# Attention outputs and sums of the third diagonal step, formed together with those of the fourth

## What is computed

```
q = (x @ Wq).reshape(B, S, N_KV, GROUP, HEAD_DIM)      # 4, 2048, 4, 4, 32
k = (x @ Wk).reshape(B, S, N_KV, HEAD_DIM)
v = (x @ Wv).reshape(B, S, N_KV, HEAD_DIM)
scores = jnp.einsum('bqkgd,bskd->bkgqs', q, k) * scale
scores = jnp.where(causal, jnp.finfo(scores.dtype).min, scores)
attn = jax.nn.softmax(scores, axis=-1)
out = jnp.einsum('bkgqs,bskd->bqkgd', attn, v)
```

## Time and profile before

| | |
|---|---|
| Median of 3 runs | 3938.41 us (3938.09 to 3940.97) |
| Profiled execution | 3937.35 us, its span 3935.6 us |
| PE busy | 3749.8 us (95%) |
| DVE busy | 2348.5 us (60%) |
| ACT busy | 1637.1 us (42%) |
| POOL busy | 1644.0 us (42%) |
| Mean granted TensorE clock | 0.973 |

### The profile page before, as it was taken

How to read it: one execution, slowest core, us unless ns; L and a number is a source line. 1 busy time by engine, 2 the same in 40 slices (tenths; PEclk the granted TensorE clock), 3 DMA queues, 4 the chain that set the end, 5 groups by cost and what they waited for, 6 DMA issues and landing times. The chain is left out here.

```text
span 3935.6 us, 71470 instructions
## 1 busy us (share of the span) xinstructions
PE 3749.8 (95%) x20752; PEld 2276.7 (58%) x20752; DVE 2348.5 (60%) x5385; ACT 1637.1 (42%) x3340; POOL 1644.0 (42%) x1412
## 2 busy tenths in 40 slices
PE   6999999999979979999999999999999999999889
PEld 5777787778854545545455444445454454544377
DVE  5454554445521128877787787778677676875144
ACT  3222222222211111555555555556555565655511
POOL 0424333242342310555555465555455455555600
PEclk9999999999999985999999999999999999999989
DMA  5232322323229972112202211210221021020086
GB/s 162 94 110 95 112 93 93 117 89 112 83 81 328 324 207 44 29 32 53 48 12 55 49 32 32 53 47 17 51 50 39 24 53 48 15 53 7 12 298 224
DMA packets 228463, 342.08 MB, mean 87 GB/s; under 512 B 65120, under 2 KB 77664, under 8 KB 228128
## 3 DMA queue, kind: packets, MB, share of 16 engines
q1 hardware_dynamic: 200480, 307.92, 25.4%
q0 software_dynamic: 17920, 12.82, 1.6%
q10 hardware_dynamic: 9728, 17.30, 1.2%
HBM read 217.28 MB, written 120.35 MB: 86 GB/s over the span
## 5 line engine op out<-in xcount | busy, mean ns | idle before, releaser
L1120 ACT ACTIVATE prb<-sps 128x512 f32<-128x512 f32 (+3 forms) x2560 | 1197.2, 538 | 903.4 <-PE sps L1238 890.8
L1153 DVE TENSOR_REDUCE mx<-mps 128x1 f32<-128x512 f32 x1536 | 1002.1, 682 | 204.0 <-PE mps L1215 204.0
L1215 PE MATMUL mps<-kst,qst 96*128 96x512 f32 (+2 forms) x2560 | 1011.2, 411 | 46.2 <-DMA kst<-k_hi_s 20.8
L1063 POOL TENSOR_TENSOR psum<-prb 128x1024 f32<-128x1024 f32 x384 | 908.5, 2381 | 292.7 <-ACT prb L1120 246.7
L1238 PE MATMUL sps<-qst,kst 97*128 97x512 f32 (+2 forms) x2560 | 967.1, 394 | 45.8 <-issue 20.4
L1238 PEld LDWEIGHTS sps<-qst,kst 97*128 97x128 f32 x2560 | 480.7, 191 | 440.9 <-ACT prb L1120 213.1
L1215 PEld LDWEIGHTS mps<-kst,qst 96*128 96x128 f32 x2560 | 502.1, 198 | 379.2 <-DVE mx L1153 202.3
L294 POOL DMA_INDIRECT tab_s<-pay,slot x384 | 380.0, 989 | 787.2 <-DVE tokf L543 667.1
L1156 DVE CUSTOM_DVE_ANT_0 mps<-mps,bias 128x256 f32<-128x256 f32 (+3 forms) x1024 | 523.3, 522 | 300.7 <-PE mps L1215 300.1
L1252 PE MATMUL ops<-prb,vst 128*32 128x512 f32 (+3 forms) x5120 | 599.5, 540 | 0.5 <-POOL prb L1053 0.5
L581 PE MATMUL acc<-x_hi,w_hi 128*128 128x512 f32 (+1 forms) x1152 | 457.1, 397 | 1.5 <-DVE x_lo L428 1.5
(11 more groups left out here) (154 smaller groups left out, 3194.6 us busy)
## 6 DMA issues: line engine op xcount, KB each, us to landing
wgu<-in_e_gu SPq DMA_DIRECT2D x32, 1408.0 KB, 7.3
qst<-q_hi_s SPq DMA_DIRECT2D x128, 256.0 KB, 4.5
x_sb<-in_x SPq DMA_DIRECT2D x16, 1024.0 KB, 7.4
xn_s<-xn SPq DMA_DIRECT2D x16, 1024.0 KB, 5.1
y_sb<-in_x SPq DMA_DIRECT2D x16, 1024.0 KB, 5.2
q_hi_s<-qk_hi SPq DMA_DIRECT2D x16, 1024.0 KB, 4.2
q_lo_s<-qk_lo SPq DMA_DIRECT2D x16, 1024.0 KB, 6.6
base<-y_sb SPq DMA_DIRECT2D x16, 1024.0 KB, 4.4
```

The costliest lines, as they stand in the source:

```text
L1063: nc.gpsimd.tensor_tensor(psum2[gi % 2][pr][:], prb[:, (2 * f + pr) % RP], prb[:, (2 * (f + 1) + pr) % RP], ALU.add).then_inc(add_done, 1)
L1120: nc.scalar.activation(prb[:, (2 * k + h // 2) % RP, h % 2, q0:CH], sps[:, (GROUP * k + h) % R, q0:CH], ACT.Exp, scale=SCALE).then_inc(exp ...
L1153: V.tensor_reduce(mx[:, h * NKT + qt, j:j + 1], mps[:, n % R, 0:wr], AX.X, ALU.max).then_inc(mred_done, 1)
L1215: M(out[:, 0:w], qst[p][0:R3, h, qt * P:(qt + 1) * P], kst[p][0:R3, k0:k0 + w], start=True, stop=True).then_inc(m_done, 1)
```

## The change

In step k TensorE formed the outputs of step k - 2. Now a list `due` says which outputs each step forms. Where step k - 2 is a third diagonal one (r = 2), its outputs are left out of step k and stand in step k + 1, ahead of those of the fourth diagonal step. For a group's last block, where k - 2 is negative, this holds across the group's end. Pieces, scores and all other engines' programs keep their order.

```
+            due = [[k - LAG] for k in range(NK)]
+            for k in range(NK):
+                if steps[k - LAG][2] == 2:
+                    due[k + 1] = due[k] + due[k + 1]
+                    due[k] = []
+
             def group(bg, p, nxt, prev=True):
...
-                    if k >= LAG:
-                        output(bg, p, k - LAG)
-                    elif prev:
-                        output(bg - 1, 1 - p, NK + k - LAG)
+                    for o in due[k]:
+                        if o >= 0:
+                            output(bg, p, o)
+                        elif prev:
+                            output(bg - 1, 1 - p, NK + o)
```

## The result

The changed kernel takes 3947.9 us (median of 17 runs, 3944.11 to 3948.85), the kernel before 3937.16 in the same runs (17, 3933.94 to 3943.71). The ratio is 1.0025 with a 95% interval of 1.0018 to 1.0032: 7 to 13 us slower, 10.7 by the medians. The profiled execution took 3948.48 us with a span of 3946.7.

A forecast was written before the change was run, and what follows sets the result against it. TensorE was taken as the attention stage's bound on average, VectorE and ScalarE following closely. Per group 0.27 + 0.24 + 0.17 - 0.07 = 0.61 us, together 9.2 us, gave 3947.5 us, range 3930 to 3956.

The forecast's parts named there:

- The price of a stretch: Attention stage, TensorE: one stretch of outputs costs 0.33 us beyond its columns; 63 merged would give 21 us.
- only the switches count: Rival for the merged blocks: VectorE and ScalarE keep up, so 21 us faster, 3917; chance 0.12.
- the crossing: Steps 0 and 1, last block of the group before: gain of 0 to 0.14 us, taken as 0.07.
- VectorE cannot follow nine pieces: Third block, steps 24 and 25: TensorE waits 0.60 us for VectorE against 0.33 saved, a loss of 0.27.
- ScalarE first in the first block, then the reciprocal: Steps 4 and 5: scores wait for exponentials, then a piece for VectorE behind its reciprocal; 0.35 us lost.
- what step 6 gives back: First block: step 6 regains about 0.18 us as VectorE would be ahead, leaving a net loss of 0.17.
- the prediction's better bound: Steps 0 and 1: step 2 comes 6.36 us after step 0, now 6.50, a gain of 0.14.
- The sum: Whole kernel: 0.61 us lost per group, 8.5 for fourteen groups, 0.68 for the first: 9.2 us slower.
- A: Rival for the merged runs: followers keep up and TensorE's saved switches alone decide; 21 us faster, 3917; chance 0.12.
- B: Rival for the merged blocks: waits and saved switches about cancel as later steps use VectorE's lead; 3934 to 3942; chance 0.18.
- C: Rival for the merged runs: every wait costs its full restart, 16 us more, 3964; chance 0.10.
- the 11 waits: TensorE's waits in the first three blocks' merged runs; at most a whole restart of 0.10 us more in each.

The follow-up runs named there:

- the written-out pair: TensorE's attention-stage loop over pairs of groups written out in the kernel before and in the changed kernel: 4097.02 us apart, 4107.44 us merged.

## Why the prediction was right

**The price of a stretch, 0.33 us.** Right, and shown where nothing else stands in the way: 0.34, 0.31 and 0.29 us won in the third, second and first block once the followers are fast. Of the 21 us of "only the switches count" the three blocks' share, some 14, is there; for the crossing no run freed it.

**VectorE cannot follow nine pieces.** Right. Piece by piece the prediction's working gave the seventh a start that counts as 3.16 and the eighth one of 3.77; the trace has them at 3.06 and 3.66 from the first score, each with the restart of 0.10 behind. The ninth was put at 4.24 and starts at 4.23. The length of the run is met too, 6.00 against 5.99. With VectorE fast the loss turns into the gain: that is the experiment that shows the cause, not only the agreement.

**ScalarE first in the first block, then the reciprocal.** Right in both parts and in what step 6 gives back (0.20 measured, 0.18 predicted). VectorE's shortened reductions alone left a loss of 0.09 there, ScalarE's shortened exponentials took it away.

**The crossing.** The prediction gave it a gain of 0 to 0.14 us, taken as 0.07. In the even groups the sign was wrong: a loss of 0.03. The step that failed there is VectorE's start. The prediction has VectorE start a piece 0.44 us behind its matmul and gives the fourth piece of this run no start of its own, but there it is 0.65:

```profile
2380.66 0.79 PE L1215 MATMUL mps<-kst,qst 96*128 96x256 f32 x3
...
2381.31 0.30 DVE L1156 CUSTOM_DVE_ANT_0 mps<-mps,bias 128x128 f32<-128x128 f32 x1 [0.30 <-PE mps L1215]
```

It did so before as well, with outputs behind that piece; it is the same without them. From there on VectorE goes through the other eight pieces with hardly a pause, and TensorE waits for it. In group 1 VectorE starts the fourth piece 0.47 us behind its matmul, and the crossing ends sooner:

```profile
1690.47 0.50 PE L1238 MATMUL sps<-qst,kst 97*128 97x512 f32 x1
...
1692.00 1.71 PE L1215 MATMUL mps<-kst,qst 96*128 96x256 f32 x5
...
1696.82 0.39 PE L1238 MATMUL sps<-qst,kst 97*128 97x256 f32 x1
```

```profile
1692.47 0.30 DVE L1156 CUSTOM_DVE_ANT_0 mps<-mps,bias 128x128 f32<-128x128 f32 x1
```

Steps 0 and 1 take 6.35 us there, before 6.50: the 0.14 of the prediction's better bound, to 0.01. The 0.18 us between the two starts of the fourth piece is also what lies between a loss of 0.03 and a gain of 0.15. Why VectorE is late in the even groups and not in the odd ones stays open. Over 14 groups the prediction had 1.0 us won, the written-out pair shows 0.9; as it came from a loss in one half of the groups and a larger gain in the other, that agreement is luck.

**The sum.** 9.2 us were predicted, the steps of the written-out pair give 9.0. The runs of the case say 10.7 (7.1 to 12.6) and the written-out pair's 10.4, and neither is fine enough to show that anything is missing. The forecast of 3947.5 us lies 0.4 from the measured 3947.9, closer than its working earns: the median of 3 runs that it started from was 1.2 us above the median of 17, and 9.2 on top of the latter gives 3946.4. Two small slips of the working cost nothing: 3938.41 + 9.2 is 3947.6, and the second block's 5.87 against 5.62 is a loss of 0.25, not 0.24.

**The rivals.** A falls with the kernel in which the third block alone is merged. B, a VectorE that gives its lead back, holds in the first block only, as its idle 1.07 us before step 26 shows. C, a full restart at each of the 11 waits, would have cost 16 us more; the records show restarts where a piece waited, which the prediction's working had already counted.

**What I had not priced.** The low clock. One loop pass in the changed kernel and the same one in the kernel before, in the stretches behind TensorE's gap, with the columns of the earlier trace rows:

```profile
2517.10:2527.30 10.20, 9.72 (x53) 7.15 (x53) 5.68 (x24) 4.35 (x8) 1.63 (x4) 0.50 0.17 47
```

```profile
2513.00:2516.40 3.40, 3.40 (x16) 2.30 (x19) 1.43 (x8) 2.39 (x4) 0.53 (x2) 0.50 0.34 93
2516.40:2523.20 6.80, 6.22 (x52) 3.88 (x49) 5.15 (x21) 3.71 (x10) 1.51 (x4) 1.00 0.13 22
```

A granted clock of 0.50, the 1.2 GHz level, for 10.2 us after, for 3.4 us before. In the profiled executions it sums to 64.9 us against 37.5 in the stage, and groups 0 to 14 together are 14.9 us longer, some 6 us more than the 9.0 of the steps at full clock. How much of it is left in the median of 17 runs can't be told: 10.7 with the loop and 10.4 without agree, but either may be off by 3 us or more. The kernel with the crossing left apart shows that it can also reach 10 us, and why it is long in one kernel and short in another stays open.

## What to carry to other kernels

A pause of one engine may be the time in which the others catch up; before a switch or a gap is taken out of a busy engine, work out buffer by buffer whether the consumers can keep the pace over the longer run that this makes. Read waits of TensorE as distances from start to start, not as idle time: the record of a matmul that waits is only 0.1 us longer. Where low clock follows the end of a loop's pass, as here, compare kernels with that loop written out, or the clock's few us may stand in the place of the change's. And compare more than one kind of group: half of these showed the crossing as a loss, the other half as a gain.

## What the runs showed of the hardware

TensorE's loop over two groups costs about 3.4 us at each pass: between the last matmul of a pass and the first of the next there is no work and no wait that the profile shows, and the gap went when the loop was written out for TensorE alone.

```profile
2239.14 0.49 PE L1238 MATMUL sps<-qst,kst 97*128 97x512 f32 x1 [3.06 <-issue]
```

Writing the loop out removed this gap and all low clock between the first and last group, and made the kernel before 0.71% faster (0.58 to 0.84). The table of pieces also proved steep: taking seven of 160 pieces from six steps and giving them to seven others, with the pieces in between moved along, cost 22 us by the medians (16 to 32).
